# First attention: score matmuls listed by row half, in a new order of the words

## The reference, cut to what matters

```
q, k, v = proj(Wq), proj(Wk), proj(Wv)            # of layernorm(x), 16 heads of 16
q, k = rope(q), rope(k)
scores = einsum('bhqd,bhkd->bhqk', q, k) / sqrt(16) + causal
ctx = einsum('bhqk,bhkd->bhqd', softmax(scores), v)
x = x + ctx @ Wo.T
```

## Time and profile before

| what | us |
|---|---|
| three runs | 2585.28, 2593.52, 2594.16 |
| median | 2593.52 |
| span of the profiled execution | 2593.8 |

### The profile page before, as it was taken

The page is one execution under the profiler, slowest core; times in us unless marked ns, Lnnn a source line. Parts: engine busy times, 40 slices in busy tenths (PEclk is TensorE's granted clock), DMA queues, the critical chain, the costliest instruction groups (busy, mean ns, idle before and its releaser), DMA issues. The chain is left out here.

```text
span 2593.8 us, 49497 instructions
## 1 busy us (share of the span) xinstructions
PE 2499.8 (96%) x16744; PEld 2090.6 (81%) x16744; DVE 1829.9 (71%) x3962; ACT 1391.2 (54%) x2455; POOL 395.4 (15%) x301
## 2 busy tenths in 40 slices
PE   7998898899999999999999999999999999999999
PEld 6864444688888888888888888888877888888888
DVE  6776777476776776767777777777777677676673
ACT  5424556455555555555555555555555555555553
POOL 0030000011211221311101011011001221222120
PEclk9997999899999999999999999999999999999999
DMA  4064331000000000000000000000000000000000
GB/s 166 17 147 67 51 43 44 33 11 24 33 32 1 32 32 0 21 0 21 21 2 21 1 21 21 1 21 21 1 33 1 33 33 27 7 33 32 0 2 30
DMA packets 19133, 73.80 MB, mean 28 GB/s; under 512 B 3344, under 2 KB 8208, under 8 KB 15632
## 3 DMA queue, kind: packets, MB, share of 16 engines
q1 hardware_dynamic: 18960, 71.78, 9.7%
HBM read 61.02 MB, written 10.49 MB: 28 GB/s over the span
## 5 line engine op out<-in xcount | busy, mean ns | idle before, releaser
L391 PEld LDWEIGHTS ps<-w,hid 128*128 128x128 f32 x5376 | 699.2, 191 | 58.0 <-DVE rb L472 13.8
L391 PE MATMUL ps<-w,hid 128*128 128x256 f32 x5376 | 719.8, 284 | 2.1 <-DVE rb L472 1.5
L356 PE MATMUL ps<-xT,w 128*128 (+1 forms) x2688 | 703.5, 397 | 2.8 <-ACT xT L417 2.8
L556 DVE TENSOR_TENSOR hid<-gel,hid 128x512 fp32r<-128x512 f32 x448 | 402.3, 908 | 334.7 <-ACT hid L432 326.6
L426 ACT ACTIVATE gel<-ps,b 128x512 f32<-128x512 f32 x448 | 306.9, 685 | 550.2 <-issue 542.1
L356 PEld LDWEIGHTS ps<-xT,w 128*128 128x128 f32 x2688 | 478.0, 190 | 81.5 <-issue 3.2
L432 ACT ACTIVATE hid<-gel 128x512 fp32r<-128x512 f32 x448 | 272.9, 622 | 0.0
L941 PE MATMUL ps<-pT,v_sb 128*128 128x512 f32 (+3 forms) x1152 | 262.2, 358 | 2.8 <-DVE pT L1065 2.8
L915 PE MATMUL ps<-k_sb,q_sb 128*128 128x512 f32 (+3 forms) x1152 | 251.5, 351 | 0.6 <-DVE q_sb L1083 0.5
L1054 DVE TENSOR_REDUCE negmax<-ps 128x1 f32<-128x128 f32 (+7 forms) x256 | 192.2, 751 | 76.0 <-PE ps L918 74.7
L1015 ACT ACTIVATE pT<-ps 128x512 fp32r<-128x512 f32 (+3 forms) x384 | 178.9, 489 | 104.0 <-PE ps L928 103.7
(11 more groups left out here) (144 smaller groups left out, 2858.8 us busy)
## 6 DMA issues: line engine op xcount, KB each, us to landing
wraw<-in_wffn SPq DMA_DIRECT2D x12, 2048.0 KB, 7.5
wraw<-in_w_a SPq DMA_DIRECT2D x8, 1280.0 KB, 5.4
qk_dram<-rope_hl SPq DMA_DIRECT2D x16, 512.0 KB, 3.4
xT<-qk_dram SPq DMA_DIRECT2D x48, 128.0 KB, 5.5
x<-in_x SPq DMA_DIRECT2D x4, 512.0 KB, 8.1
xb<-in_wffn SPq DMA_DIRECT2D x2, 1024.0 KB, 7.1
rot<-in_rot SPq DMA_DIRECT2D x1, 2048.0 KB, 15.6
xb<-in_wffn SPq DMA_DIRECT2D x1, 2048.0 KB, 14.0
```

The costliest lines, as they stand in the source:

```text
L356: last = nc.tensor.matmul(ps[:, HPS + j % 4, :], w[par][:, wp, 0, k * HIDDEN + j * PART:k * HIDDEN + (j + 1) * PART], xT[:, xp, k, bass.ds ...
L391: last = nc.tensor.matmul(y_ps[:, t, :], hid[:, hp, j % 4, t * PART:(t + 1) * PART], w[par][:, wp, 1, j * DIM:(j + 1) * DIM], start=j == 0 ...
L556: nc.vector.tensor_tensor(hid[:, 1, j % 4, :], gel[:, j % 4, :], hid[:, 0, j % 4, :].bitcast(f32), ALU.subtract).then_inc(low_done, 1)
```

## The change: what it does

Each U and T word now has a further index a and covers one row half. The matmuls, masks, reduces and exponentials are the same, as are waits in number: a U half waits for its own ring bank; T waits before half a = 0 and signals ACT after half a = 1. Masks of a U or T word on the diagonal follow (or, in the two steps with two blocks, precede) the score matmuls of their own half; before they alternated between the halves. The order of the words within a group is written as a string of letters, applied to each of the eight groups; T, U and A take the next item of their kind.

```
--- before
+++ after
+        ORDER_A0 = ("TTUTTUAUU TTUTTA TUTTTUUAU TTTTUU "
+                    "TTTUUTACA TUTTTUUAUU TTUTTC TUUTAUTT "
+                    "TTUUAUUTT TTUUUUATUTNU TTTTUUAUUA TTTTUUAUU ").replace(" ", "")
...
             for letter in ORDER_A0 * GROUPS:
                if letter == "T":
                    i, (p, a) = tile // 4, divmod(tile % 4, 2)
                    if tile % 4 == 0:
                        todo += late.pop(i - 1, [])
                        todo += begin.get(i - (GROUPS - 1) * len(TILE_STEPS), [])
                    todo.append(("T", i // len(TILE_STEPS), i % len(TILE_STEPS), p, a))
                    tile += 1
                elif letter == "U" and row < len(halves) * GROUPS:
                    todo.append(("U", row // len(halves), *halves[row % len(halves)]))
                    row += 1
                    if row % len(halves) == 0:
                        todo.append(("J", row // len(halves) - 1))
                elif letter == "N" and turned < GROUPS:
                    todo.append(("N", turned))
                    turned += 1
                elif letter == "A" and behind:
                    behind -= 1
                elif letter == "A":
                    weigh()
                elif letter == "C" and lagging:
                    context()
...
-            def rows(g, u, p):
+            def rows(g, u, p, a):
...
                 def masks(n):
                     for part in range(2 if diagonal else 0):
-                        for a in range(2):
-                            last[a] = causal(a, dst[a][:, (n + 1) * width - PART:(n + 1) * width], 0, part,
-                                             n == 0 and part == 0 if together else None)
+                        last = causal(a, dst[:, (n + 1) * width - PART:(n + 1) * width], 0, part,
+                                      n == 0 and part == 0 if together else None)
+                    return last
...
-            def tiles(g, s, p):
+            def tiles(g, s, p, a):
...
-                wait(pe, t_exp, i - 1)
-                dst = [ps[:, 2 * p + a, 0:width] for a in range(2)]
-                for a in range(2):
-                    stack = slice(a * HROW, a * HROW + STACK + 2)
-                    last = nc.tensor.matmul(dst[a], QK[g % 4][1][stack, p, kt * PART:(kt + 1) * PART],
-                                            QK[g % 4][0][stack, p, qc * CHUNK + q0:(qc + 1) * CHUNK],
-                                            start=True, stop=not diagonal)
+                if a == 0:
+                    if s == 0:
+                        pe.wait_ge(mx_loaded[g % 4][p], 64 * (g // 4 + 1))
+                    wait(pe, t_exp, i - 1)
+                dst, stack = ps[:, 2 * p + a, 0:width], slice(a * HROW, a * HROW + STACK + 2)
+                last = nc.tensor.matmul(dst, QK[g % 4][1][stack, p, kt * PART:(kt + 1) * PART],
+                                        QK[g % 4][0][stack, p, qc * CHUNK + q0:(qc + 1) * CHUNK],
+                                        start=True, stop=not diagonal)
                 for part in range(2 if diagonal else 0):
-                    for a in range(2):
-                        last = causal(a, dst[a], 1, part)
-                last.then_inc(t_ready, 1)
+                    last = causal(a, dst, 1, part)
+                if a == 1:
+                    last.then_inc(t_ready, 1)
```

More of the change, by code:

```diff
@@ L1277, in rows_of @@
                 if ROW_STEPS[u]:
-                    todo.append(("U", g, u, p))
+                    todo.extend(("U", g, u, p, a) for a in range(2))
                 if j % T_GROUP == T_GROUP - 1:
@@ L1313, in plan_a0 @@
                      8: [("Y", 6)], 10: [("R", 1, 0), ("R", 1, 1)]}
[L1315 to L1340, removed]
@@ new lines, in plan_a0, with weigh @@
+            halves = [(u, p, a) for u in range(len(ROW_STEPS)) if ROW_STEPS[u] for p in range(2) for a in range(2)]
+            tile, product, turned, behind, lagging = 0, 0, 1, AV_LAG, []
+            def weigh():
+                nonlocal product
+                g, s = divmod(product, len(TILE_STEPS))
+                qc, kt = TILE_STEPS[s]
+                product += 1
+                todo.append(("A", g, s))
+                if (qc, kt) in ((0, 3), TILE_STEPS[-1]):
+                    todo.append(("X", g, qc))
+                    lagging.append(("C", g, qc))
@@ L1341, in plan_a0 @@
+            while product < steps:
+                weigh()
+            while lagging:
+                context()
             for i in sorted(late):
@@ L1345, in build @@
         PLAN = plan_a0()
-        RING = [item for word in PLAN if word[0] in "UNCEOR"
-                for item in ([(*word, a) for a in range(2)] if word[0] == "U" else [word])]
+        RING = [word for word in PLAN if word[0] in "UNCEOR"]
         BY_BOTH = [item for item in RING if item[0] in "NER"]
@@ L1454, in rows @@
-                if not together:
-                    masks(0)
-                for a in range(2):
-                    last[a].then_inc(ring_ready, 1)
-            def tiles(g, s, p):
+                    last = nc.tensor.matmul(dst[:, n * width:(n + 1) * width],
+                                            QK[g % 4][0][stack, p, qt * PART:(qt + 1) * PART],
+                                            QK[g % 4][1][stack, p, kc * CHUNK:kc * CHUNK + width],
+                                            start=not together, stop=together or not diagonal,
+                                            skip_group_check=together)
@@ L1460, in tiles @@
+                if diagonal and not together:
+                    last = masks(0)
+                last.then_inc(ring_ready, 1)
+            def tiles(g, s, p, a):
                 qc, kt, q0, width, diagonal = tile_step(s)
                 i = T_GROUP * g + 2 * s + p
-                if (g, s, p) == (0, 0, 0):
+                if (g, s, p, a) == (0, 0, 0, 0):
                     pe.wait_ge(rope_taken, N_PIECES)
-                if s == 0:
-                    pe.wait_ge(mx_loaded[g % 4][p], 64 * (g // 4 + 1))
@@ L1543, in act_attend_a0, with tiles @@
         def act_attend_a0(act):
-            def tiles(g, s, p):
+            def tiles(g, s, p, a):
                 width = tile_step(s)[3]
                 step = len(TILE_STEPS) * g + s
+                if a == 0:
+                    return
                 act.wait_ge(t_ready, 2 * step + p + 1)
```

61 lines of the change are left out of this document (44 added, 17 removed).

## The result

The changed kernel takes **2612.32 us** (median of 7 runs, 2596.9 to 2619.62) against 2590.68 for the kernel before (7 runs beside it). The ratio on record is 1.0066, 95% interval 1.0044 to 1.0088; it is not the quotient of the two medians, which is 1.0084. Forecast were 2586 and a range of 2568 to 2605. A second set, 12 runs against 29, gave 2611.45 against 2591.61: 1.0067 [1.0037, 1.0097]. It is slower by 0.7%, just over what can be told from no change.

What follows compares the result with a forecast made beforehand. In the first attention, a loop of head, N to split, and small DMAs was taken as the bound. Loops 1 to 5 gain 8.0 us, loop 6 0.5, loop 0 loses 1.2: -7.3, forecast 2586 us, range 2568 to 2605.

Steps and rivals of the forecast that it cites:

- the third rival: First attention's loops: halves left alone bring the low clock, 10.1 us more per low loop, 2596 or 2606; chance 0.17.
- the two low loops: Two more first-attention loops at 1.2 GHz, 10.1 us more each, giving 2606 us.
- What closes it: T of pair 1 waits for eight small maxima DMAs, landing 6.55 us after DVE's split, in a 31.13 us loop.
- Waits in the head: From T of pair 1 to N: PE's waits for free ring banks shrink from 2.8 us to 0.3.
- Step 9 in the head: N now stands behind all of step 9, whose two pairs add 0.55 us to the head.
- lost partners: Row halves without a partner in the head: 38 places against 33, three at 0.34, adding 1.0 us.
- fewer changes of shape: Array shape changes in the head drop from 12 to 10, saving 0.15 us each, 0.3 in all.
- The end of N: From N to the end of DVE's split: 1.47 us falls to 1.1.
- Loop after: Full-clock loop of 29.5 us (head 21.85, then 1.1 and 6.55) against 31.13, gaining 1.6; bounds 28.05 and 32.0.
- Two streams: Row halves run as separate in-order streams, so half 1's matmul may pass half 0's queued masks; masks by half cost nothing.
- the second rival: Halves start in program order: diagonal pairs start 0.30 us apart, loop 36.5 us, total 2636 us; chance 0.08.
- Signs: If right: loops 29.0 to 30.0, PE's wait at T 1 us or more, DVE over 85% busy in the head.

Runs made afterwards that it cites:

- e1: The changed kernel timed again, nothing further changed: 2611.45 us, ratio 1.0067 to the kernel before.
- e7: Changed kernel with the two halves of each word side by side again, N, A and C at their new places: 2578.45 us, ratio 0.9950 to before.
- e2: Changed kernel's split words and masks by half, but in the letter order of the kernel before, halves next to each other: 2581.31 us, ratio 0.9967 to before.
- e13: Changed kernel, halves spread, with two extra small DMAs lengthening the wait at T of pair 1 in groups 1 to 7: 2662.32 us, ratio 1.0280 to before.
- e14: Changed kernel with halves joined, N, A and C at new places, and two extra small DMAs lengthening the wait: 2611.59 us, ratio 1.0080 to before.
- e6: Changed kernel with eight unread matmuls run where PE stood idle before T of pair 1: 2583.83 us, ratio 0.9981 to before.
- e12: Split words in the order of the kernel before, plus two extra small DMAs lengthening PE's wait, groups 1 to 7: 2605.13 us, ratio 1.0062 to before.
- e9: Changed kernel with the first nine letters of a loop joined, the rest spread: 2589.95 us, ratio 0.9973 to before.
- e10: Changed kernel with the first nine letters kept spread, halves of the rest joined: 2577.05 us, ratio 0.9945 to before.
- e3: Changed kernel with head pair 1's four maxima DMAs issued from GpSimd's queue from group 1 on: 2579.26 us, ratio 0.9954 to before.
- e5: Split words in the order of the kernel before, with head pair 1's four maxima DMAs on GpSimd's queue: 2574.83 us, ratio 0.9942 to before.

## Why the prediction was wrong

**The step that failed is the clock.** The sum carried the low-clock time of the kernel before over unchanged; more of it was the third rival, at 0.17. Its condition was right, that halves left alone bring the low clock; that they do so because they "load the array less" is argued, no run measures it. Wrong was its price: a loop wholly at the low clock cost 49.31 - 29.94 = 19.4 us, not 10.1. The 41.24 of loop 0 are no measure of that: only 31.3 us of that loop lie in the low stretch of the earlier trace rows, and it holds fewer words than loop 1 (318 matmuls against 329), so 31.12 need not be its length at full clock. Wrong too was the weight of the reason against it: groups 1 and 2 had stayed at 1.00 with their waits. But those rows show joined halves, so they speak for that loading of the array alone. The change kept the idle time at T and changed what surrounds it, and the 83 us more at 1.2 GHz in the mean run cost 31 us, more than the 20 of the two low loops to which the range reached. The part of the sum that was worked out, a gain of 7.3 us, came at the same clock: 6.5 by the loops, 8 to 11 by the lines.

Shown: with nearly the same wait, spreading the halves costs clock (e1 against e7, with e2 at the wait of e1; e13 against e14); with the same words, idle time at the wait costs clock (e1 against e6; e2 against e12; e7 against e14; e1 against e13). By the traces the idle time is where the clock mostly falls: of 17 falls in loops 1 to 6 of before, the changed kernel, e1, e12, e13 and e14, 15 come during the wait at T of pair 1 or within 2.1 us of its end; those at 318.2 us of before and 374.7 of e1 come 13 and 21 us behind it. That the spread halves mainly make the low clock last is suggested, not shown. The stays in those loops are 17.1 and 47.8, then 47.8, 3.4 and 3.4, then 20.5, 95.6 and 68.3 us with spread halves (the changed kernel, e1, e13), and 3.4 to 20.5 in all eight with joined ones (e12, e14); but these are single executions, and e7's stay of 64.8 from the start of loop 0, with joined halves, speaks against. The means over all runs show stays and number of falls only together. Not settled: which of the spread halves count (e9, e10), and why the waits of loops 2 and 3 of the changed kernel passed while those of loops 1 and 5 didn't, and what ends a stay.

**The loop, point by point.**
- *What closes it.* Right: T waits for the DMAs 6.55 us after DVE's split, before and after; shortening that chain (e3, e5) shortened the loop.
- *Waits in the head.* Right in kind, wrong in size. I counted 2.8 us from distances and took 0.3 for after. PE is idle for 23.11 - 21.43 = 1.68 us in the head of the earlier trace rows, of which the table of waits names 1.0 + 0.3 = 1.3 as waits for DVE, and for none of the 22.39 after. So the idle time is worth 1.7, not 2.5. In the two answers here the last column is the longest wait; before, then after:

```profile
PE ps L1449 <- DVE nmx L1616: 1.0, 3, 0.5
PE ps L1470 <- DMA q_own<-nmT: 0.8, 1, 0.8
PE ps L1380 <- DVE nmx L1616: 0.3, 1, 0.3
```

```profile
PE ps L1490 <- DMA q_own<-nmT: 0.9, 1, 0.9
```

- *Step 9 in the head* +0.55, *lost partners* +1.0, *fewer changes of shape* -0.3. With the first as forecast, 23.11 - 1.68 + 0.55 = 21.98, and 22.39 was measured: 0.4 is left for the other two together, where 0.7 was forecast. It can't be divided further, and it also holds waits that PE's busy time hides: in e2 the two halves of the row word at 279.90 start 0.5 apart though PE has no idle time there. The errors of this step and of the last offset each other in part: the head was forecast at 21.85.
- *The end of N.* 1.1 forecast, 1.00 measured.
- *Loop after.* 29.5 forecast, 29.94 measured, inside the 29.0 to 30.0 given; gain 1.2 in place of 1.6.
- *What brings the gain.* I gave it to the order, which puts turned halves between row halves. e2 shows that the split does it: its head is 22.14 against 23.11, and PE's table of waits names none for DVE any more, even with the halves side by side. The likely reason is that a half asks for one bank where a pair asked for two; that is argued. The order adds 0.1 and brings the low clock.
- *Two streams.* Right, against the rule that matmuls are "pc-monotone in start AND end" (the Trainium skill, "TensorE: Matmul & The Clock Gate", What overlaps and what doesn't), which this trace does not bear out for matmuls of different row halves. In the changed kernel two masks of one half stand between the two score matmuls of a diagonal word, and yet the two start together: at T(3, 0, pair 1) both stand in one line of the timeline at 303.09, their four masks in the next at 303.43, and the two of T(3, 1, pair 0) both start at 305.39. The 0.30 of the second rival is in neither.
- *Signs.* T's idle time grew from 0.8 to 0.87 only, and DVE is busy 18.40 of the head's 22.39, 82%, not over 85%. The clock row below 1.00 in group 1 was named as the sign of the third rival.

## What to carry to other kernels

Where PE stands idle once a loop at full clock, look at which clock it keeps before reordering what surrounds that point: here such a loop was one edit away from the low clock, and rows of the old order didn't vouch for the new one. Price a low stretch from a loop that is low throughout, or by the low microsecond. Time several runs, note each one's mean clock, and compare kernels at the same clock as well as by medians: here that separated a gain of some 10 us from a loss of some 30. Split a change first (one bank per word without moving anything kept 0.3% of gain; joined words and a second queue for the small DMAs made it 0.7%).

## What the runs showed of the hardware

- The clock fell beside 0.9 us of idle time once in a loop of 30 us (PE busy 29.07 of 29.94 where it did not fall): in the changed kernel in loops 1 and 5, not in 2 and 3. PE's busy time beside the wait was alike with and without a fall (2.49 and 2.51 against 2.52 and 2.53 us of 3.40). What PE executes in the loop matters: spread halves against joined ones, mean clock 0.9719 against 0.9878 (e1, e7) and 0.9525 against 0.9778 (e13, e14).
- A low stay can outlast much fully busy time: 47.8 us with PE busy 47.80, 95.6 with 95.16 (e13), and with joined halves 64.8 with 64.73 (e7).
- Matmuls that nobody reads, run in a wait (e6), cost nothing in the loop and gave back 0.013 of mean clock, 28 us in the median.
- Of the eight small DMAs from one queue, each issue takes 0.67 us. With four of them on GpSimd's queue (e3) the chain no longer sets the loop: PE has no wait left at T, and the loop is 28.85 us.
